# A two-layer graph network on one core: gate biases negated earlier, pair 0's closing steps spread over pair 1's units, transposes between the tiles of the first dense products

## The reference, cut to what matters

```python
def L0(x, adj, W_sa, a_sa, W_g, b_g, Wa, ba, Wb, bb):          # x: 3327 x 256, adj: 3327 x 3327 of 0 and 1
    ts = adj @ x
    attn_a = sigmoid(concat([ts, x], 1) @ Wa.T + ba)
    attn_b = sigmoid(concat([ts, x], 1) @ Wb.T + bb)
    h = x @ W_sa
    scores = (h @ a_sa[0, :256])[:, None] + (h @ a_sa[0, 256:])[None, :]
    e = where(adj != 0, exp(-leaky_relu(scores, 0.01)), 0)
    x_a = (e / (e.sum(1, keepdims=True) + 1e-5)) @ h
    x_b = adj @ (x @ W_g) + b_g
    return sigmoid(attn_a * x_a + attn_b * x_b)
x = x + L0(relu(layernorm(x)), ...)
h = relu(layernorm(x)); deg = max(adj.sum(-1), 1)
x = x + relu((((adj + I) / deg) @ h + h) @ W1 + b1)     # dinv * a_hat * dinv, dinv = deg ** -0.5 per row
```

## Time and profile before

| | |
|---|---|
| runs of the kernel | 609.41, 609.82 (median), 611.63 us |
| the profiled execution | 611.8 us, its span 610.0 us |
| busy of the span | TensorE 593.4 us, VectorE 425.2, ScalarE 362.4, GpSimd 255.5 |
| mean granted clock of TensorE | 0.993 of full |

### The profile page before, as it was taken

The page is one execution under the profiler, slowest core; times in us unless marked ns, Lnnn a source line. Parts: engine busy times, 40 slices in busy tenths (PEclk is TensorE's granted clock), DMA queues, the critical chain, the costliest instruction groups (busy, mean ns, idle before and its releaser), DMA issues.

```text
span 610.0 us, 13250 instructions
## 1 busy us (share of the span) xinstructions
PE 593.4 (97%) x5265; PEld 508.4 (83%) x5265; DVE 425.2 (70%) x811; ACT 362.4 (59%) x878; POOL 255.5 (42%) x361
## 2 busy tenths in 40 slices
PE   7889998999999999999999999999999999999996
PEld 5446687888888888888888888888888888888886
DVE  6897885999998999899989989988753121111111
ACT  3687667797887979797979788979642000000000
POOL 3664313554453435343525276313132374435433
PEclk8999999899999999999999999999999999999999
DMA  8908399957566565647474745010400486546401
GB/s 198 225 3 113 111 134 249 203 83 182 94 150 121 123 134 110 146 98 162 81 177 67 190 52 79 2 19 1 130 2 18 113 318 215 174 157 193 144 20 35
DMA packets 55801, 73.60 MB, mean 121 GB/s; under 512 B 20027, under 2 KB 47933, under 8 KB 54331
## 3 DMA queue, kind: packets, MB, share of 16 engines
q0 software_dynamic: 28544, 22.15, 26.5%
q1 hardware_dynamic: 24754, 46.42, 23.5%
q10 hardware_dynamic: 2441, 4.20, 2.2%
HBM read 69.31 MB, written 22.16 MB: 150 GB/s over the span
## 4 chain that ended last, share of the span: by engine, by line
PE 82%; DVE 5%; DMA 4%; issue 4%; POOL 4%; ACT 2%; ACTq 0%; POOLq 0%; DVEq 0%
PE accE L786 11%; PE accE L788 11%; PE accE L787 11%; PE accA L764 10%; PE accA L765 10%; PE accA L831 7%; PE accA L830 7%; PE accE L830 4%; PE accE L831 4%; DMA stage<-in_adj_dram 3%; POOL stage L369 1%; DVE bst L933 1%; PE pw L803 1%; PE accA L847 1%; PE pw L805 1%
## 5 line engine op out<-in xcount | busy, mean ns | idle before, releaser
L786 PE MATMUL accE<-HI,Z 128*128 128x257 f16 x676 | 185.2, 274 | 2.4 <-DVE wm L1078 2.1
L788 PE MATMUL accE<-HI,E 128*128 128x257 f16 x676 | 184.8, 273 | 0.0
L787 PE MATMUL accE<-LO,Z 128*128 128x256 f16 x676 | 184.7, 273 | 0.0
L549 ACT ACTIVATE Z<-LO,sr 128x256 f32<-128x256 f32 x338 | 151.4, 497 | 35.6 <-PE accE L788 35.6
L764 PE MATMUL accA<-HI,adjT 128*128 128x260 f16 x676 | 154.0, 273 | 0.0
L765 PE MATMUL accA<-LO,adjT 128*128 128x258 f16 x676 | 154.0, 273 | 0.0
L558 ACT ACTIVATE Z<-Z,sr 128x256 f32<-128x256 f32 x338 | 150.1, 496 | 0.2
L1034 DVE TENSOR_TENSOR Z<-adjT,Z 128x512 f32<-128x512 bf16 x169 | 127.0, 751 | 17.1 <-ACT Z L558 16.1
L1040 DVE TENSOR_TENSOR E<-Z 128x512 bf16<-128x512 f32 x169 | 129.0, 763 | 5.8
L369 POOL DMA_DIRECT2D stage<-in_adj_dram x96 | 59.3, 649 | 93.0 <-DVE adjT L1026 88.6
L831 PE MATMUL accA<-LO,adjT 128*128 128x256 f16 x416 | 91.6, 273 | 0.0
(11 more groups left out here) (127 smaller groups left out, 721.0 us busy)
## 6 DMA issues: line engine op xcount, KB each, us to landing
adjT_store<-adjT SPq DMA_DIRECT2D x11, 1664.0 KB, 6.3
stage<-in_adj_dram POOLq DMA_DIRECT2D x48, 192.0 KB, 5.0
stage<-in_adj_dram POOLq DMA_DIRECT2D x36, 224.0 KB, 5.2
adjT<-adjT_store SPq DMA_DIRECT2D x7, 896.0 KB, 6.0
adjT<-adjT_store SPq DMA_DIRECT2D x7, 768.0 KB, 6.0
stage<-adjT_store SPq DMA_DIRECT2D x4, 896.0 KB, 6.4
stage<-adjT_store SPq DMA_DIRECT2D x4, 768.0 KB, 5.8
out_dram<-late ACTq DMA_DIRECT2D x11, 256.0 KB
```

What stands on the lines that cost most here:

```text
L549: ins = act.activation(Z[:, n % RING, v], slw[:, m], ACT.Relu, bias=sr99[:, t:t + 1], scale=1.0 - SLOPE)
L786: pe.matmul(dst[:, 0:D + 1], zhi, HI[:, t, 0:D + 1], start=(t == 0), stop=False)
L787: pe.matmul(dst[:, 0:D], zhi, LO[:, t, 0:D], start=False, stop=False)
L788: ins = pe.matmul(dst[:, 0:D + 1], zlo, HI[:, t, 0:D + 1], start=False, stop=(t == TILES - 1))
```

## The change

The negation for `nbias` moves on GpSimd from behind `load_adj(3, 0)` to behind `load_adj(0, 1)`. On ScalarE and VectorE pair 0's closing steps move into pair 1's loop, at u = 1 to 7, and pair 1's own `row_sums(0)`, `gate_args(1)` and `gates(1)` (with `gate_exp(1)`) move back by one or two units. In the front the transposes of pairs 1 and 2 and the first projection stand between the two tiles of `dense(0)` and `dense(1)`; the projections, the evacuations by halves and `take_scores` of the first pairs move with them. Nothing is computed differently.

```diff
@@ GpSimd @@
             load_adj(0, 1)
+            pool.wait_ge(bias_in, 32)
+            pool.tensor_scalar(nbias[:], bias2[:], -1.0, None, ALU.mult).then_inc(nbias_ok, 1)
             loads = {6: (1, 0), 7: (1, 1), 11: (2, 0), 12: (2, 1)}
...
             load_adj(3, 0)
-            pool.wait_ge(bias_in, 32)
-            pool.tensor_scalar(nbias[:], bias2[:], -1.0, None, ALU.mult).then_inc(nbias_ok, 1)
             with_bias(0)
@@ ScalarE: turned(i), first_halves(i) becomes first_half(i, e) @@
                 act.wait_ge(hT_ps, i + 1)
+                if 2 <= i <= 3:
+                    act.wait_ge(proj, i - 1)
                 if i >= 2:
                     act.wait_ge(dn_ps, 2 * i - 2)
...
             for s in range(PAIRS + 7):
                 if s == 0:
-                    first_halves(0)
+                    first_half(0, 0)
                 if s + 1 < PAIRS:
                     turned(s + 1)
+                if s == 0:
+                    first_half(0, 1)
                 if s + 2 < PAIRS:
                     norm(s + 2)
                 if 0 <= s - 6 < PAIRS:
                     expo(0, s - 6)
                 if 0 < s < PAIRS:
-                    first_halves(s)
-                if s == 1:
+                    first_half(s, 0)
+                    first_half(s, 1)
+                if s == 2:
                     left_first()
...
-            act.wait_ge(srw_ok, PAIRS)
-            act.activation(el[:], srw[:, :, 3], ACT.Exp, scale=SLOPE).then_inc(el_ok, 1)
-            gate_exp(0)
-            gated_b(0)
...
                     if u == 7:
                         half_tanh(m - 1)
-                    if u == 9:
+                    if m == 1 and u == 1:
+                        act.wait_ge(srw_ok, PAIRS)
+                        act.activation(el[:], srw[:, :, 3], ACT.Exp, scale=SLOPE).then_inc(el_ok, 1)
+                    if m == 1 and u == 3:
+                        gate_exp(0)
+                    if m == 1 and u == 5:
+                        gated_b(0)
+                    if u == (10 if m == 1 else 9):
                         gate_exp(m)
@@ TensorE: dense(i), and the front's loop @@
                 for e in range(2):
+                    if i <= 1 and e == 1:
+                        turn(i + 1)
+                    if i == 1 and e == 1:
+                        project(0)
                     if i >= 1:
                         pe.wait_ge(lo_ok, 2 * i - 1 + e)
...
                 dense(s)
                 if s == 0:
-                    turn(1)
-                    project(0)
+                    keep_busy(5)
+                if s == 1:
                     spread_weights(2, 4, 2)
-                    keep_busy(4)
-                if s == 1:
+                    turn(3)
+                    project(1)
+                if s == 2:
+                    project(2)
                     widen_first()
-                if s + 2 < PAIRS:
+                if 2 <= s and s + 2 < PAIRS:
                     turn(s + 2)
...
-                if s + 1 < PAIRS:
+                if s >= 2 and s + 1 < PAIRS:
                     project(s + 1)
@@ VectorE @@
             row_stats(2)
+            second_half(0, 0)
+            minus_mean(2)
+            turned_second(1)
+            second_half(0, 1)
             dve.wait_ge(w1_in, 16)
             largest(3, 4)
             on_diagonal(2, 4)
-            second_halves(0)
-            minus_mean(2)
+            row_stats(3)
             take_scores(0)
-            turned_second(1)
-            row_stats(3)
-            diagonal_first()
-            scales(2, 4, 2)
             row_stats(4)
             minus_mean(3)
+            scales(2, 4, 2)
+            diagonal_first()
             for s in range(1, PAIRS + 6):
-                if s < PAIRS:
+                if 2 < s < PAIRS:
                     take_scores(s)
...
                 if s < PAIRS:
-                    second_halves(s)
+                    second_half(s, 0)
+                    second_half(s, 1)
+                if s <= 2:
+                    take_scores(s)
...
-            turn_adj(2, 0)
-            gate_args(0)
-            gates(0)
...
                 for u in range(PAIRS):
-                    if u == 4:
+                    if m == 1 and u == 1:
+                        gate_args(0)
+                    if m == 1 and u == 2:
+                        turn_adj(2, 0)
+                    if m == 1 and u == 3:
+                        gates(0)
+                    if u == (6 if m == 1 else 4):
                         row_sums(m - 1)
-                        if m == 1:
-                            turn_adj(2, 1)
+                    if m == 1 and u == 7:
+                        turn_adj(2, 1)
...
-                    if u == 6:
+                    if u == (8 if m == 1 else 6):
                         gate_args(m)
...
-                    if u == 9:
+                    if u == (11 if m == 1 else 9):
                         gates(m)
```

More of the change, by code:

```diff
@@ L524, in first_weights, with first_half @@
                 act.activation(dst, src, ACT.Copy, scale=winv[:, (0, 1, 3)[k]:(0, 1, 3)[k] + 1]).then_inc(whi_ok, 1)
-            def first_halves(i):
+            def first_half(i, e):
                 src = dn[:].rearrange("p (e k d) -> p e k d", e=2, k=2)
[L528 to L531, removed]
+                act.wait_ge(dn_ps, 2 * i + e + 1)
+                dst = bass.AP(HI[:].tensor, (2 * i + e) * HIW, [[TILES * HIW, P], [G0, 2], [1, D]])
+                act.activation(dst, src[:, e], ACT.Copy).then_inc(hi_ok, 1)
             def left_first():
@@ L1003, in diagonal_first, with second_half @@
                 ins.then_inc(diag_ok, 1)
[L1005 to L1011, removed]
+            def second_half(i, e):
+                dve.wait_ge(hi_ok, 2 * i + e + 1)
+                first = bass.AP(HI[:].tensor, (2 * i + e) * HIW, [[TILES * HIW, P], [G0, 2], [1, D]])
+                dve.tensor_tensor(LO[:, 2 * i + e, 0:2 * D].rearrange("p (k d) -> p k d", k=2),
+                                  bank(dn, e).rearrange("p (k d) -> p k d", k=2), first,
+                                  ALU.subtract).then_inc(lo_ok, 1)
             def turn_adj(m, c):
```

## The result

The changed kernel is slower. Its median is 612.58 us (22 runs, 610.86 to 614.79) beside 610.41 us of the kernel before (22 runs): a ratio of the two sets of runs of 1.003 with the interval 1.0019 to 1.0042, or 1.8 us (the medians alone lie 2.2 us apart). Timed again with the experiments it gave 1.0029 (1.0018 to 1.004). I had forecast 2.1 us less.

What follows compares the result with a forecast made beforehand. The prediction took TensorE as the bound, busy 487.79 of 488 us from 112 to 600 us. 2.22 + 1.67 - 1.5 - 0.3 = 2.1 us less, so 609.8 - 2.1 = 607.7 us; eight in ten: 605.9 to 610.3.

Steps and rivals of the forecast that it cites:

- Together 3.89 us: TensorE before unit(1,0): 2.22 us idle waiting for wm plus 1.67 us at half speed behind it, all gained.
- A new wait of 1.5 us: TensorE at unit(2,0): wm(1) comes at 134.29, wanted at 132.91, so 2.4 of 3.89 us stay.
- rival D: Pair 1: GpSimd's with_bias(0) blocks VectorE, pushing row_sums(0) and gates(1) by 1.6 us; 609.3 us, chance 0.08.
- I take a loss of 0.3 us: The front: later take_scores(2) delays dense(3); between a gain of 0.3 and a loss of 0.8 us.
- that of the clock: The front: a clock fall behind the gap near 20 us would cost 0.2 us, as VectorE waits until 27.7 anyway.
- where I had allowed 0.5: Sign of being right: VectorE at the first turn of pair 0 within 0.5 us of before.
- Rival E: load_adj(3,0), issued 3 us later, lands late; VectorE waits 2.6 us, unit(2,0) 4.1, then half speed; 612.0 us, chance 0.07.
- Rival C: The 1.5 us gap at unit(2,0) is followed by half speed, another 1.67 us; 609.4 us, chance 0.13.
- Rival B: No wait at unit(2,0), VectorE's chain to gates(1) being 1.5 us shorter; 606.2 us, chance 0.27.

Runs made afterwards that it cites:

- a1_again: The changed kernel, unchanged, profiled again: 33.85 us from dense(0) to the first neighbours, 91.07 from there to unit(2,0).
- h1_nbias_late: The changed kernel with nbias directly ahead of load_adj(3, 0) on GpSimd: ratio to the kernel before 1.0031.
- b1_again: The kernel before, unchanged, profiled a second time: 611.65 us.
- e2_front: The kernel before with only the front's part of the change: ratio to the kernel before 1.0014.
- g2_both: The changed kernel with row_sums(0) at u = 5, gates(1) at u = 9, pair 2's second halves ahead of minus_mean(3): ratio to the kernel before 0.9988.
- g1_hTl: e2_front with pair 2's second halves ahead of minus_mean(3), scales and the diagonal on VectorE: ratio to the kernel before 0.9996.

## Why the prediction was wrong

**The step that failed first: "Together 3.89 us".** Rows and sum were right for the execution that they came from, and the change does remove that gap. But I took one execution as the kernel, and subtracted its gap from the median of three. Its VectorE had waited 1.09 us for a load; that made the gap long, and the long gap made the clock fall. In four others with the old pair 1 the gap is 1.13 to 1.21 us at full clock. The term measures 1.26 us.

**"A new wait of 1.5 us" at unit(2,0)** came, and where I put it: 1.42 us from start to start. Mis-sized was the whole term, for unit(1,11) lost 0.74 before it; together 2.2, and 91.08 - 88.79 = 2.3 us in all. gates(1) started 74.77 us after the first neighbours, where I had 118.4 - 44.12 = 74.28. unit 11 was split at 79.9, where I had 122.96 - 44.12 = 78.8. Part of that is GpSimd's sum in with_bias, for which I had allowed time of its own and none of VectorE's: the mask beside it took 1.29 us (126.17) and not 0.69, and the split beside the sum of with_bias(0) 1.75 (103.61). So rival D named a true mechanism; it is the sum that does it, not the whole of with_bias. wm of pair 0 was 0.7 us later than I had it (59.87 after the first neighbours against 59.13), still in time.

**"I take a loss of 0.3 us"** for the front. I named norm(3) as what turn(3) would wait for and put the idle time at 2.2 us. It also waits for the second halves of pair 2, which the change puts behind the scales and the diagonal on VectorE, and the idle time was 3.4 us. I had not followed that semaphore through VectorE's new order. But it accounts for 0.54 us only. norm(3) itself started as I had it (8.4 to 9.0 us after dense(0) in the changed kernel's profiles, where I had 21.3 - 12.54 = 8.8); in the first profile TensorE was also ready for turn(3) 0.7 us sooner (7.0 us after dense(0) against 20.2 - 12.54 = 7.7). The mis-sized price is that of the clock, for which I allowed 0.2 us: it fell in dense(2), later VectorE waited 1.26 us for the halves, and between a1_again and h1_nbias_late 1.6 us of a longer dense(2) came through to the first turn in full. VectorE came to its first turn 28.3 to 28.9 us after dense(0) in seven of eight profiles with the old front and 29.9 to 31.0 after it in four of four of the changed kernel, where I had allowed 0.5. The runs give 0.9 us for the front (0.1 to 1.6).

**The sum, corrected.** 1.26 gained, 2.3 lost at pair 1, 0.9 lost in the front: 1.9 us more, measured 1.8. (The base was low as well: 610.41 us in 22 runs, where three had given 609.82.) Rival E (the load (3,0) late) didn't happen: the turn of (3,0) at 115.33 had no wait. Rival C didn't either: the clock stayed full behind unit(2,0), over a gap of 1.5 us. Rival B was the wrong way. None of the rivals had the one that decided: that most of the prize was not there in the usual execution. All cases had the same 3.89 in them, so the range, 605.9 to 610.3, was too narrow.

**Open** is how the front's 0.9 us divides in the timed runs between the order on VectorE, the clock and the landing of x. The profiles give the clock up to 1.6 us, x up to 2.8 us and the order 0.54 us of one wait; none alone was large enough to be told in the timed runs.

## What to carry to other kernels

Before the size of a gap becomes a gain, profile the kernel two or three times more and compare the same stretch, the gap and the clock behind it; look for a wait on a transfer ahead of the gap. The total of the profiled execution doesn't tell: all three here lay 1.5 to 2.0 us above the median, for three different reasons. Take first the smallest edit that removes the cause that the trace names (here one negation behind a load on an in-order engine), and see what is left for the rest of the plan. When a step is moved ahead of another on an engine, list every semaphore that the displaced step sets, and follow each to who waits for it.

## What the runs showed of the hardware

- TensorE's clock stayed full behind gaps (start to start) of 1.05 to 1.56 us, of 2.2 us in b1_again (22.21 to 24.41) and, ahead of turn(3), of 3.0 us in e2_front (20.21 to 23.19) and 3.6 in g2_both (21.40 to 25.02). It fell behind 2.33 us in the first execution of before, behind 2.75 us in g1_hTl (22.62 to 25.37), and at turn(3) of the changed kernel and h1_nbias_late behind 3.2 to 3.7. The length of one gap doesn't decide it. The Trainium skill (TensorE: Matmul & The Clock Gate, Why this matters for your kernels) warns of long idle gaps between bursts; the falls behind 3.2 to 3.7 us agree, the full clock behind 3.6 us in g2_both doesn't.
- A GpSimd operation on two tensors held one of VectorE's, also on two, to about its own end (the profile's spans on GpSimd are rough): beside 103.54 (1.27 us) a split that began 0.07 later took 1.06 more than its 0.69; beside 125.64 a mask that began 0.53 later took 0.60 more. Two multiplies by a scalar took 2.40 at 101.06, 0.06 behind the start of a split, and 1.83 at 123.72 with VectorE idle: there GpSimd paid. A mask at 102.89, within the second of them, kept its 0.69. The Trainium skill (SBUF — State Buffer, Who interferes with whom) has the shared port as an exclusive lock, the later one waiting; the sums and the first multiply agree with it, the mask at 102.89 doesn't.
- The program's start differs from execution to execution by up to 2.9 us (dense(0) at 12.54 to 15.46), more than the whole change.
